# A new hand-written issue order for all engines of a cross-attention kernel

## The chip, the cores and the metric

The kernel runs on one core of a Trainium2 chip. The metric is the device time of one execution in microseconds (us), from start to end of the program. An execution is also profiled, and the profile gives the span from its first to its last instruction.

## What is computed

The reference, cut to what matters (B = 32 batches, 512 query rows and 512 context rows of 512 features, 16 heads of 32, all float32):

```python
qn  = layer_norm(x, q_norm_g, q_norm_b)
kvn = layer_norm(ctx_1024, kv_norm_g, kv_norm_b)
Q = (qn @ Wq).reshape(B, 512, 16, 32).transpose(0, 2, 1, 3)
K = (kvn @ Wk).reshape(B, 512, 16, 32).transpose(0, 2, 1, 3)
V = (kvn @ Wv).reshape(B, 512, 16, 32).transpose(0, 2, 1, 3)
attn = softmax(einsum('bhqd,bhkd->bhqk', Q, K) / sqrt(32))
ctx = einsum('bhqk,bhkd->bhqd', attn, V).transpose(0, 2, 1, 3).reshape(B, 512, 512)
out = x + gelu(ctx @ Wo + bo, approximate=False)
```

## The kernel before, in words

The program is one software pipeline, unrolled over the batches -1 to 32. A batch has four steps, one for each group of four heads (a "unit"). Each engine walks its own list of short names, `ORDER[engine][step]`, and waits on semaphores where a name needs another engine's result. So the lists alone set which work stands ahead of which on an engine. `known(b)` and `valid(b)` drop names that have no batch to work on. In batch -1, the head, only loads, normalisation, weight preparation and the first products exist; `PLAN_OF_HEAD` sorts its steps 2 and 3 a little differently.

The names on TensorE (PE):

- `q`, `k`, `v`, `o`: one sixth of a projection of 512 columns, two matmuls each (12 for a projection, because each float32 operand is split in a high and a low part of type fp32r, L868). In step s, `q` and `k` belong to the unit two steps ahead.
- `s`: one score block of the next unit, which is only reduced to its row maximum (L896, evicted by VectorE, L718, also named `s`). `st`: one transposed score block of the current unit (L888, evicted by ScalarE with the exponential, L575, also named `st`). Sixteen of each in a step, all in one rotation of four PSUM banks (`score`): a score matmul waits until the score block four places before it has been evicted.
- `m`: transposes the maxima when VectorE has reduced all 16 blocks (`md`, L777). It starts a short chain: ScalarE `mh` (L625), VectorE `ml` (L783), ScalarE `mx` four times (L629), and then the next step's first `st` may run.
- `pv`: 16 column-tiled matmuls, probabilities times V (L916), two in a step. `z`: 8 matmuls for the softmax sums (L859), which wait for six additions on GpSimd (`add`, L487).
- `x`: four transposes of a normalised tile (L956), eight in step 1. `x` on ScalarE and VectorE are the copies out of PSUM (L600, L694).

The projections, `x`, `m` and `z` share three PSUM banks (`gen`), taken in rotation in the order in which they are listed; the next user of a bank waits for the last one's eviction.

The other names: `ln`, `la`, `lv` (VectorE, L737 to L749) and `ln` (GpSimd, L503, L506) are the layer norm's statistics, and `norm` (ScalarE, L596) applies them. `q` and `k` on ScalarE (L606, L620) and VectorE (L696) evict the two parts of a projection, which SyncE then spreads by DMA into `q_stack` and `k_stack` (`rq`, `rk`). `rz` copies zero rows into `q_stack`. `ob` (VectorE, L759) adds the output bias, `gelu` (ScalarE, L592) follows, `res_add` (GpSimd) adds the residual, `store` and `res` are its transfers. `zt`, `zr`, `zb`, `cn` normalise the context, `split` cuts it in its two parts. `stack_used` tells that all `st` of a step are done, so that a stack's slot may be written again.

Of the kernel before, what the change touches and what calls it, by code (L numbers as in the profile page):

```python
# [19 lines left out]
NU = HEADS // HU  # L20
# [40 lines left out]
    ),  # L61
    "act": (
# [4 lines left out]
    ),  # L67
    "dve": (
        "s ln s*2 ln s la ln q ln s la s la zt zr lv s zb lv*2 cn la s*9 md ml ln k ob",
        "ln la lv la ln q lv zt zr zb ln la x s lv s cn lv s*2 k x s x la s lv x*2 s*4 x s*2 x ob s*2 x s*2 "  # L70
        "md ob ml",
        "s*5 ob s*2 zt s zr zb s cn s*4 k s*3 md q ml",
        "k zt zr zb cn s*2 q s*14 md ml",
    ),
    "pool": (
        "ln*3 split add*6 ln*3 res_add",
        "ln add ln add*3 res_add add res_add add split",
        "add*6 split res_add",
        "split add*6",
    ),  # L80
    "sp": (
        "load*6 rz rq load*2 rk store res",
        "rz rq rk",
        "store res rz rk rq store first_res",
        "rk store rq rz first_res",
# [94 lines left out]
def build(nc, x, ctx_in, q_g, q_b, kv_g, kv_b, wq, wk, wv, wo, bo, out):  # L180
    B = x.shape[0]
    zero_rows = nc.dram_tensor("zero_rows", (SHIFTS, HU * D), F32).ap()
    with ExitStack() as es:
# [21 lines left out]
        res = sb("res", [P, 2, D])  # L205
# [27 lines left out]
        ctx_ps = ps("ctx")  # L233
# [60 lines left out]
        def known(b):  # L294
            return isinstance(b, int)
# [5 lines left out]
        def valid(b):  # L301
            return not known(b) or 0 <= b < B
# [81 lines left out]
        def _(sp):  # L384
# [23 lines left out]
            def batch(b):  # L408
                PLAN = plan_of(b)
                for s in range(NU):  # L410
# [4 lines left out]
                    for kind, n, part in PLAN["sp"][s]:  # L415
                        if kind == "load" and valid(b + 1):
                            load_tile(b + 1, n)
                        if kind == "rz" and valid(b2):
# [5 lines left out]
                        if kind in ("rq", "rk") and valid(b2) and not (kind == "rq" and known(b) and (b, s) == (-1, 2)):  # L424
                            which = kind[1]
                            wait(sp, free[which], NU * b2 + u2 + 1)
                            wait(sp, stack_used, NU * b2 + u2 + 1)
# [577 lines left out]
```

## Time and profile before

| | us |
|---|---|
| median of 3 runs | 3231.49 |
| lowest, highest | 3231.26, 3232.49 |
| the profiled execution's own time | 3231.49 |
| its span, first to last instruction | 3229.7 |
| mean granted TensorE clock | 0.997 of full speed |

The profiled execution is the median itself, and 1.8 us of it lie outside the span. In the profile a group of instructions is named by its line and by what it writes and reads. "Idle before" is the time for which the engine stood still just ahead of an instruction, and the arrow names what ended it.

### The profile page before, as it was taken

How to read it: one execution, taken by the hardware profiler on the slowest of the kernel's cores; microseconds unless marked ns; L12 is line 12 of the kernel's file. 1: busy time of each engine (PE TensorE's matmuls, PEld its weight loads, DVE VectorE, ACT ScalarE, POOL GpSimd, SP SyncE). 2: the span in 40 equal slices, each digit the busy share in tenths (PEclk: the TensorE clock that was granted, in tenths of full speed). 3: DMA queues.
4: the chain of work that ended last, by engine and by line, in shares of the span. 5: the costliest groups of instructions: out<-in, count | busy, mean ns of one | idle time of the engine just before them, and what ended most of it. 6: DMA issues, size and time to landing. Idle time of an engine off the chain costs nothing.

```text
span 3229.7 us, 50112 instructions
## 1 busy us (share of the span) xinstructions
PE 3196.3 (99%) x16611; PEld 2148.0 (67%) x16611; DVE 2274.2 (70%) x4769; ACT 2306.6 (71%) x3985; POOL 2318.6 (72%) x1544
## 2 busy tenths in 40 slices
PE   8999999999999999999999999999999999999998
PEld 5566666666666666666666666666666666666664
DVE  6677677677677776776776777766767767777664
ACT  4677767777767777677777677776777776777765
POOL 2677677777777777777777777777777777777775
PEclk9999999999999999999999999999999999999999
DMA  4445445345444354453454444544534544544442
GB/s 147 101 104 129 115 119 133 95 115 137 115 115 120 104 130 115 120 133 95 115 136 116 115 119 105 130 115 121 131 95 115 138 115 114 121 105 128 115 102 79
DMA packets 193010, 376.85 MB, mean 117 GB/s; under 512 B 22625, under 2 KB 22641, under 8 KB 188658
## 3 DMA queue, kind: packets, MB, share of 16 engines
q1 hardware_dynamic: 192288, 372.86, 45.2%
q8 instruction: 134, 2.20, 0.3%
q14 instruction: 122, 1.00, 0.1%
q10 hardware_dynamic: 466, 0.80, 0.1%
HBM read 138.42 MB, written 33.82 MB: 53 GB/s over the span
## 4 chain that ended last, share of the span: by engine, by line
PE 98%; DVE 1%; ACT 1%; issue 0%; DMA 0%; ACTq 0%; POOL 0%
PE gen L868 43%; PE score L896 15%; PE score L888 15%; PE ctx L916 15%; PE gen L859 4%; PE gen L956 3%; PE gen L978 1%; DVE maxes L718 1%; PE score L800 0%; ACT probs L575 0%; PE gen L849 0%; ACT q_stack L629 0%; PE score L849 0%; ACT tok L596 0%; PE score L827 0%
## 5 line engine op out<-in xcount | busy, mean ns | idle before, releaser
L487 POOL TENSOR_TENSOR probs<-probs 128x1024 f32<-128x1024 f32 x762 | 1806.5, 2405 | 430.1 <-PE ctx L916 426.2
L718 DVE TENSOR_REDUCE maxes<-score 128x1 f32<-128x512 f32 x2048 | 1304.0, 681 | 267.8 <-PE score L896 256.7
L575 ACT ACTIVATE probs<-score 128x512 f32<-128x512 f32 x2048 | 1083.5, 606 | 229.7 <-PE score L888 219.9
L896 PE MATMUL score<-k_stack,q_stack 128*128 128x512 f32 x2048 | 728.7, 404 | 0.8 <-DVE maxes L718 0.2
L888 PE MATMUL score<-q_stack,k_stack 128*128 128x512 f32 x2048 | 713.9, 401 | 6.4 <-ACT q_stack L629 5.1
L896 PEld LDWEIGHTS score<-k_stack,q_stack 128*128 128x128 f32 x2048 | 380.0, 188 | 216.2 <-issue 81.1
L888 PEld LDWEIGHTS score<-q_stack,k_stack 128*128 128x128 f32 x2048 | 377.8, 188 | 185.6 <-ACT probs L575 42.4
L916 PE MATMUL ctx<-probs,v_sb 128*32 128x512 f32 x4096 | 492.4, 598 | 0.6 <-ACT probs L575 0.5
L868 PE MATMUL gen<-cT,w_k 128*128 128x512 f32 x1536 | 451.9, 399 | 0.1
L868 PE MATMUL gen<-xT,w_q 128*128 128x512 f32 x1536 | 444.0, 395 | 0.0
L868 PE MATMUL gen<-w_v,cT 128*128 128x512 f32 x1536 | 443.8, 390 | 0.0
L868 PE MATMUL gen<-w_o,ctx_hl 128*128 128x512 f32 x1488 | 401.5, 394 | 0.0
L503 POOL TENSOR_TENSOR rstd<-var_eps,minus_half 128x1 f32<-128x1 f32 x256 | 142.1, 555 | 322.5 <-DVE neg_mean L749 322.5
L696 DVE SCALAR_TENSOR_TENSOR k_nat<-gen,bias_k,k_nat 128x512 fp32r<-128x512 f32 x128 | 95.8, 749 | 357.9 <-ACT k_nat L620 357.9
L629 ACT ACTIVATE q_stack<-max_hl,chunk_mask 32x512 fp32r<-32x512 f32 x512 | 326.3, 706 | 29.7 <-DVE max_hl L783 28.2
L868 PEld LDWEIGHTS gen<-cT,w_k 128*128 128x128 f32 x1536 | 283.4, 191 | 80.1 <-DVE q_nat L696 27.0
L868 PEld LDWEIGHTS gen<-w_v,cT 128*128 128x128 f32 x1536 | 288.8, 188 | 62.6 <-issue 0.8
L868 PEld LDWEIGHTS gen<-xT,w_q 128*128 128x128 f32 x1536 | 288.7, 190 | 59.0
L868 PEld LDWEIGHTS gen<-w_o,ctx_hl 128*128 128x128 f32 x1488 | 274.9, 188 | 56.7
L916 PEld LDWEIGHTS ctx<-probs,v_sb 128*32 128x32 f32 x4096 | 109.3, 109 | 230.6 <-issue 206.8
L514 POOL TENSOR_TENSOR ctx_hl<-ctx_n,ctx_hl 128x512 fp32r<-128x512 f32 x128 | 164.9, 1288 | 99.8 <-ACT ctx_hl L581 99.7
L586 ACT ACTIVATE v_sb<-gen 128x512 f32<-128x512 f32 x128 | 76.1, 594 | 220.7 <-PE gen L868 220.7
(89 smaller groups left out, 2720.9 us busy)
## 6 DMA issues: line engine op xcount, KB each, us to landing
k_stack<-k_nat SPq DMA_DIRECT2D x384, 256.0 KB, 4.2
q_stack<-q_nat SPq DMA_DIRECT2D x381, 256.0 KB, 5.1
tok<-in_x SPq DMA_DIRECT2D x132, 256.0 KB, 6.0
tok<-in_ctx SPq DMA_DIRECT2D x128, 256.0 KB, 6.3
q_stack<-zero_rows SPq DMA_DIRECT2D x128, 256.0 KB, 3.3
res<-in_x SPq DMA_DIRECT2D x124, 256.0 KB, 2.6
out<-res SPq DMA_DIRECT2D x124, 256.0 KB, 2.5
probs<-in_L_xattn_Wq SPq DMA_DIRECT2D x1, 1024.0 KB, 8.5
```

The source lines that it names most:

```text
L487: pool.tensor_tensor(probs[:, c + 1, heads], probs[:, c + 1, heads], probs[:, c, heads], ALU.add).then_inc(pool_added, 1)
L503: pool.tensor_tensor(rstd[:, n:n + 1], var_eps[:, n:n + 1], minus_half[:], ALU.pow).then_inc(ln_rstd, 1)
L514: pool.tensor_tensor(ctx_hl[:, 1, up], ctx_n[:], raw(ctx_hl[:, 0, up]), ALU.subtract).then_inc(ctx_split, 1)
L575: act.activation(probs[:, n, part, :], score_at(s, "st", i)[:], ACT.Exp, scale=SCALE).then_inc(exp_done, 1)
L629: act.activation(q_stack[SROW:P, u1 % 2, :, P * n:P * (n + 1)], raw(max_hl[SROW:P, :]).unsqueeze(1).to_broadcast([SHIFTS, HU, P]), ACT.Ide ...
L718: dve.tensor_reduce(maxes[:, u1 % 2, SROW + i:SROW + i + 1], score_at(s, "s", i)[:], AX_X, ALU.max, negate=True).then_inc(max_done, 1)
L859: mm = pe.matmul(bank[DH * j:DH * (j + 1), :], ones[:, 0:DH], probs[:, c, j, :], start=(i == 0), stop=(i == len(chunks) - 1))
L868: mm = pe.matmul(bank[:, :], stationary(hs, c), moving(hm, c), start=(i == 0), stop=(i == len(TERMS) * NC - 1))
L888: pe.matmul(score_bank(pe, b, s, "st", i)[:, :], k_stack[:, s % 2, part, P * n:P * (n + 1)], q_stack[:, s % 2, part, :], start=True, stop= ...
L896: pe.matmul(score_bank(pe, b, s, "s", i)[:, :], q_stack[:, u1 % 2, n, P * part:P * (part + 1)], k_stack[:, u1 % 2, n, :], start=True, stop ...
L916: mm = pe.matmul(ctx_ps[DH * j:DH * (j + 1), :], v_sb[:, c, lo:lo + DH], probs[:, c, j, :], start=(c == 0), stop=(c == NC - 1))
L956: mm = pe.matmul(bank[:, P * c:P * (c + 1)], tok[:, n, P * c:P * (c + 1)], ident[:], start=True, stop=True, is_transpose=True)
```

## The change

All engines' lists are written anew. Per step nearly the same names stand in them; their sequence differs. One `o` goes from step 1 to step 2 on TensorE, one `ln` and one `lv` from step 1 to step 0 on VectorE, one `res_add` from step 2 to step 1 on GpSimd; on SyncE stores and residual loads change steps. The name `rz` is gone: the transfer of zero rows is issued where `rq` stands, ahead of the q restack, with one wait on `stack_used` for both. The copy of the output bias on VectorE, once in the program, moves from the start of step 0 of batch 0 into `prepare`, which is called ahead of the first `q` or `k` of a step.

```diff
     "pe": (
-        "q*3 v*2 s q s q s v st*2 v st q st s st v st*2 v s v*2 st s st z s st*2 v st v*2 s*2 v st s pv st s "
-        "st s k st s*2 o s*2 pv m k*5 o*3",
-        "o st*4 o st q*4 st q*2 st*2 x z k st k st k st k st s k s x k st s*2 st x pv st s st s x*2 pv s*3 x "
-        "s x s o s o*3 x o*2 s*2 o*4 s*2 o*4 m",
-        "o s o s*4 o s k o s k*2 st*2 k st z s q st*2 q st*2 k s st k st*2 s st q s pv s st*3 q st s q s st q "
-        "s*2 pv m",
-        "k*3 q k q k v st*2 k st*2 q st*2 v st q st q*2 st*4 z st*3 s v*2 st s*2 pv s*3 v s v s v*2 s*3 v s "
-        "v*2 s*2 v s*2 pv m",
+        "q*3 v q*2 v q v st*2 v*2 s st v st s st v*2 st s st s z v st*3 s v*2 st*2 s st k v s*4 pv st s st*2 o s "
+        "st s k s*2 pv m k o*2 k o k*2",
+        "o st*2 o st*3 q st q*4 st q st*3 z x k*3 x st*2 x st k*2 s k st s st*2 pv s x s x s x s pv s x s*2 o*3 "
+        "s*2 x o s o*2 s o s o*2 s o s o*3 m",
+        "o*4 s o s k s k s st k s st z st s st s st q st q st s s st*2 k st*3 k s st k st*4 pv s*2 q s q s*2 q s*2 q "
+        "pv m",
+        "k q k v q v k*2 st*3 k st*2 q st*2 k q st q st q st*2 z st*4 v st v s*3 pv s*2 v s*2 v s*2 v s v s*2 v*2 "
+        "s*2 v s*2 v pv m",
     ),
     "act": (
-        "st*5 q st*4 v st*3 split st v st*3 norm*2 mh norm mx*4 k",
-        "st*5 gelu q st*4 x st*3 x st norm st k x norm st*2 x*2 norm*3 x*3 gelu mh gelu mx*4 split",
-        "gelu st*11 k st*5 q split mh mx*4",
-        "st*7 k st*8 q split st v*2 mh mx*4",
+        "q st*4 v st*8 norm v split norm*2 st*4 mh mx*4 k",
+        "st*6 gelu q st x st*2 norm st*4 x k st*2 norm x norm st x*2 norm x norm x*2 gelu mh gelu mx*4 split",
+        "gelu st*12 k split st*4 q mh mx*4",
+        "st*6 k st*5 q st*4 split st v*2 mh mx*4",
     ),
     "dve": (
-        "s ln s*2 ln s la ln q ln s la s la zt zr lv s zb lv*2 cn la s*9 md ml ln k ob",
-        "ln la lv la ln q lv zt zr zb ln la x s lv s cn lv s*2 k x s x la s lv x*2 s*4 x s*2 x ob s*2 x s*2 "
-        "md ob ml",
-        "s*5 ob s*2 zt s zr zb s cn s*4 k s*3 md q ml",
-        "k zt zr zb cn s*2 q s*14 md ml",
+        "q s ln s*2 la ln lv s ln s la*2 zt s zr lv zb s cn ln lv s la s*3 lv s*5 md ml ln*2 k ob",
+        "ln la*2 q zt lv*2 x la zr ln zb cn lv s la x k lv s x s*2 x*2 s*2 x s*3 x s*2 x s ob s*4 md ob ml",
+        "s ob s*6 zt s zr zb s cn s k s*7 md q ml",
+        "k zt zr zb cn q s*16 md ml",
     ),
     "pool": (
-        "ln*3 split add*6 ln*3 res_add",
-        "ln add ln add*3 res_add add res_add add split",
-        "add*6 split res_add",
+        "ln*3 split add*6 res_add ln*3",
+        "ln*2 add*5 res_add add res_add split res_add",
         "split add*6",
+        "add split add*5",
     ),
     "sp": (
-        "load*6 rz rq load*2 rk store res",
-        "rz rq rk",
-        "store res rz rk rq store first_res",
-        "rk store rq rz first_res",
+        "load*8 rq rk store res",
+        "rq rk store res store",
+        "store first_res rk rq first_res",
+        "rq rk",
     ),
...
-                        if kind == "rz" and valid(b2):
+                        if kind == "rq" and valid(b2):
...
                             wait(sp, free[which], NU * b2 + u2 + 1)
-                            wait(sp, stack_used, NU * b2 + u2 + 1)
                             if which == "q":
                                 restack(sp, u2, q_nat, q_stack, ((0, 0), (1, 0), (2, 1)), q_stacked)
                             else:
+                                wait(sp, stack_used, NU * b2 + u2 + 1)
                                 restack(sp, u2, k_nat, k_stack, ((0, 0), (1, 1), (2, 0)), k_stacked)
```

## Rows read from the trace of the kernel before

**Rows 1.** Busy time in one batch: PE, PEld, DVE, ACT, POOL; then clock, DMA share, GB/s.

```profile
1006.58:1105.40 98.82, 98.81 (x517) 66.57 (x516) 70.52 (x149) 71.71 (x124) 72.70 (x49) 1.00 0.46 118
```

**Rows 2.** TensorE's timeline in one batch of the steady stretch: start, length, what.

```profile
1006.58 0.27 PE L978 MATMUL gen<-ident,maxes 128*128 128x128 f32 x1
...
1011.50 0.61 PE L888 MATMUL score<-q_stack,k_stack 128*128 128x512 f32 x2
...
1012.73 1.06 PE L859 MATMUL gen<-probs,ones 128*32 128x512 f32 x8
1013.72 0.50 PE L896 MATMUL score<-k_stack,q_stack 128*128 128x512 f32 x1
...
1030.39 0.66 PE L888 MATMUL score<-q_stack,k_stack 128*128 128x512 f32 x2
...
1039.32 0.61 PE L896 MATMUL score<-k_stack,q_stack 128*128 128x512 f32 x2
...
1072.50 0.33 PE L978 MATMUL gen<-ident,maxes 128*128 128x128 f32 x1
...
1074.97 1.98 PE L868 MATMUL gen<-w_o,ctx_hl 128*128 128x512 f32 x8
1076.79 1.11 PE L888 MATMUL score<-q_stack,k_stack 128*128 128x512 f32 x4
...
1082.40 1.06 PE L859 MATMUL gen<-probs,ones 128*32 128x512 f32 x8
...
1105.40 0.27 PE L978 MATMUL gen<-ident,maxes 128*128 128x128 f32 x1
```

**Rows 3.** ScalarE's timeline, step 3 of that batch.

```profile
1030.92 3.54 ACT L575 ACTIVATE probs<-score 128x512 f32<-128x512 f32 x7 [0.65 <-PE score L888]
1034.48 0.69 ACT L620 ACTIVATE k_nat<-gen,bias_k 128x512 fp32r<-128x512 f32 x1
1035.07 4.25 ACT L575 ACTIVATE probs<-score 128x512 f32<-128x512 f32 x8
```

**Rows 4.** ScalarE's timeline at the start of step 2.

```profile
1010.63 0.63 ACT L581 ACTIVATE ctx_hl<-ctx_n 128x512 fp32r<-128x512 f32 x1 [0.18 <-PE gen L868]
1011.53 0.60 ACT L592 ACTIVATE act_out<-gen 128x512 f32<-128x512 f32 x1 [0.27 <-DVE gen L759]
1013.44 4.92 ACT L575 ACTIVATE probs<-score 128x512 f32<-128x512 f32 x9
```

**Rows 5.** VectorE's timeline, the last part of step 1.

```profile
1092.84 0.68 DVE L694 TENSOR_TENSOR xT<-gen,xT 128x512 fp32r<-128x512 f32 x1
...
1095.78 2.49 DVE L718 TENSOR_REDUCE maxes<-score 128x1 f32<-128x512 f32 x4 [0.27 <-PE score L896]
...
1101.04 0.70 DVE L759 TENSOR_TENSOR gen<-gen,bias_all 128x512 f32<-128x512 f32 x1 [0.38 <-PE gen L868]
...
1104.88 0.17 DVE L777 TENSOR_REDUCE maxes<-maxes 128x16 f32<-128x16 f32 x1
```

**Rows 6.** GpSimd's timeline: the six additions of step 0.

```profile
1067.67 14.19 POOL L487 TENSOR_TENSOR probs<-probs 128x1024 f32<-128x1024 f32 x6 [0.53 <-PE ctx L916]
```

**Rows 7.** VectorE's timeline in the head: first statistics, first variance.

```profile
5.56 1.28 DVE L737 BATCH_NORM_STATS2 stats<-tok 128x6 f32<-128x512 f32 x2
...
8.23 0.12 DVE L748 TENSOR_SCALAR var_eps<-moments 128x1 f32<-128x1 f32 x1
```

**Rows 8.** TensorE's timeline: head and batch 0.

```profile
12.96 1.97 PE L956 MATMUL gen<-ident,tok 128*128 128x128 f32 x8 [1.63 <-DVE xT L694]
...
17.75 1.86 PE L800 MATMUL score<-probs,norm_cols 128*1 128x512 f32 x2
...
89.66 1.75 PE L888 MATMUL score<-q_stack,k_stack 128*128 128x512 f32 x5 [1.55 <-ACT q_stack L629]
...
118.42 0.30 PE L978 MATMUL gen<-ident,maxes 128*128 128x128 f32 x1 [3.38 <-DVE maxes L777]
```

**Rows 9.** The page's DMA issues: size of one, and us to landing.

```profile
k_stack<-k_nat SPq DMA_DIRECT2D x384, 256.0 KB, 4.2
```

More of the change, by code:

```diff
@@ L689, in prepare @@
                     low_weights(3, "o", None)
+                if (b, s) == (0, 0):
+                    dve.wait_ge(bo_mm, 1)
+                    dve.tensor_copy(bias_all[:], ctx_ps[:]).then_inc(bo_ready, 1)
+                    dve.wait_ge(bo_ready, 1)
             def low_part(dst, psum, hi, done, bias=None):
@@ L705, in batch @@
                     t1, t2, tp = NU * b1 + u1, NU * b2 + u2, NU * bp + up
-                    if known(b) and (b, s) == (0, 0):
-                        dve.wait_ge(bo_mm, 1)
-                        dve.tensor_copy(bias_all[:], ctx_ps[:]).then_inc(bo_ready, 1)
-                        dve.wait_ge(bo_ready, 1)
                     for kind, n, part in PLAN["dve"][s]:
```

3 rows, old and new, of the table ORDER are left out of this document.

## The prediction, made before the changed kernel was built or run

> **What bounds the kernel now.** I read the windows first. In one batch of the steady stretch, 98.82 us long, TensorE is busy for 98.81; VectorE, ScalarE and GpSimd are busy for 70 to 73 us [rows 1]. The clock is at 1.00. So TensorE sets the time, and what it does in a batch does not depend on the sequence of its names: 192 projection matmuls, 128 scores, 8 `pv`, 4 `z`, 8 `x`, 4 `m` before and after. The counts per step differ by one `o` alone. With no wait to remove inside, a new order can hardly gain there; what it can do is make a wait. "72% busy" does not say how near that is. So I next put the timelines of the engines beside each other and looked for margins: how long before TensorE reaches a name is the result that it needs ready. They are small everywhere, some tenths of a us, and each number below is such a margin, recomputed for the new lists. Last I read the head and batch 0, where TensorE does stand still.
>
> Prices on TensorE, from rows: eight matmuls of 512 columns take 1076.79 - 1074.97 = 1.82 us, so 0.228 each: a score costs 0.23, a token of `q`, `k`, `v` or `o` (two matmuls) 0.455 [rows 2]. A `z` takes 1013.72 - 1012.73 = 0.99, and I add 0.2 for the slower start of it and of what follows (the row behind it is 0.50 long and not 0.39 as others): 1.2 [rows 2].
>
> **Terms, step by step.** All are for one steady batch; about 30 batches are full.
>
> (a) Start of a step. Behind `m` the next step's first `st` waits for ScalarE's four `mx`. Before, step 0 to 1 has 8 tokens and a `norm` between `mh` and `mx`; now 7 tokens and the `o` of step 1, so 8 again, and no `norm`. Nothing lost: 0.
>
> (b) End of step 1. The last `m` waits for 16 reductions. Before, from VectorE's third `x` at 1092.84 there stand 6 `x`, 11 `s`, one `ob` and small ones, and VectorE still idles 0.27 and 0.38 us, and `md` ends at 1104.88 + 0.17 = 1105.05, 0.35 ahead of `m` at 1105.40 [rows 5, 2]. So some 1.0 us are spare. Now 14 `s` stand behind the third `x`, at 0.60 each (four of them take 2.49 us with an end of 0.68, [rows 5]): 3 x 0.60 = 1.8 more, 0.2 less for one `la` and `lv`. TensorE needs two tokens less between the two `m`: 1105.40 - 1072.50 = 32.90 becomes 31.99. The third `x` copy comes earlier, because ScalarE's list has one `norm` less before it and no `norm` before `mx`: I add up the new ScalarE list (an exponential (3.54 - 0.6) / 6 = 0.49 [rows 3]; `x` at 0.5 and `norm` at 0.7, estimates on both sides of `k`'s 0.59) and get 18.9 us behind the first `m` where it was 1092.84 - 1072.50 = 20.3. VectorE's rest is then 14 x 0.60 + 6 x 0.60 + 0.6 + 0.2 = 12.8, ready at 31.8 for 31.99. The margin is 0.2 at best, and no idle time is left in VectorE's row of work to absorb a late copy. I take a loss of 0.1; bounds 0 and 0.5.
>
> (c) Step 3, a score bank. The third `s` ahead of the first `pv` takes the bank of the 15th `st`. Before: the first `st` starts at 1030.39, ScalarE works from 1030.92 on, seven exponentials, `k` (0.59 until the next starts), eight exponentials, and the 15th ends at 1035.07 + 4.25 = 1039.32 [rows 3]. That `s` is the second matmul of the row at 1039.32, so at 1039.55: margin 0.23 [rows 2]. The `q` eviction stood behind all of them. Now it stands ahead of the last five: 0.59 more, at `k`'s price. TensorE's path between the same two is the same set, 16 `st`, 2 `s`, 8 tokens, one `z`, again 9.16 us. ScalarE had idled in the row of eight (7 x 0.49 + 0.6 = 4.0 of its 4.25), so 0.25 is absorbed. Loss: 0.59 - 0.25 - 0.23 = 0.1, and up to 0.3 if the idle time isn't all usable. I take 0.2; bounds 0 and 0.36. The Trainium skill, "TensorE: Matmul & The Clock Gate", section "Architectural detail", says that ScalarE's and VectorE's queues are strictly first in, first out, and this rule speaks against the change: an eviction that nobody needs soon holds up those behind it. If the engine could pass `q` by, the term would be nothing; the trace shows no instruction passing another on ScalarE, and the sum goes by the rows.
>
> (d) Step 2, score banks. TensorE reaches the first `st` 1011.50 - 1006.58 = 4.92 us behind `m` [rows 2], and ScalarE's first exponential starts at 6.86, because `split`, `gelu` and a table load come first [rows 4]. Now three `s` and one `k` less and one `o` more stand ahead of the first `st`: 4.92 - 0.69 + 0.0 = 4.23. ScalarE gets earlier too: `split` waited 0.18 for the last `o`, which is now the fifth token and not behind seven `s`, and `gelu` waited 0.27; with both gone and the 0.1 to 0.2 between them the first exponential starts at 6.2 to 6.4 and ends 0.6 later, at 6.8 to 7.0. The score four places on comes at 4.23 + 3 x 0.23 + 0.455 + 1.2 + 0.23 = 6.8. Loss 0 to 0.2; I take 0.1.
>
> (e) `z` of step 1 waits for six additions: they end at 1067.67 + 14.19 = 1081.86, 0.54 ahead of `z` at 1082.40 [rows 6, 2]. Between the first `pv`, which releases them, and `z` one token less stands now: 0.54 - 0.455 = 0.09. No loss, but no room. The three other `z` lose 0.45 to 0.9 of their margins in the same way. Together with the `gelu` that moved behind a sixth exponential: 0.05, bounds 0 and 0.3.
>
> (f) SyncE. Zero rows now leave just ahead of the q restack, and the k restack has no transfer but these ahead of it in steps 1 and 3. A restack of k lands 4.2 us after its issue [rows 9], and the first `s` that reads it stands over 7 us of TensorE's work behind in every step. Hidden: 0. If that cover went it would cost the landing time less what is left of the cover, some us in a batch; nothing points there. The bias copy is at the same place in effect, since the first name in VectorE's step 0 is now `q`: 0.
>
> (g) The head. VectorE's first `lv` starts at 8.23, behind four statistics and three `la`; now behind two statistics and one `la`: two statistics at 0.6 each (two take 1.28) and small ones earlier, 1.3 us [rows 7]. All that follows it on GpSimd and ScalarE up to the first transpose moves with it. Further, the second `x` stood three places behind the first in the rotation of three banks (`x z k .. x`) and so waited 1.63 us for its copy [rows 8]; now `z x k x x` gives it another bank. I take 1.2 of that. From 17.75 on [rows 8] no gap stands in TensorE's timeline for 40 us, so what it starts earlier there counts in full: -2.5; bounds 0 (the weights come too late) and -3.5.
>
> (h) Batch 0 and the end. With no `o` to do, TensorE waits for `mx` before the first `st` of step 1 for 1.55 us and for the maxima at its end for 3.38 us [rows 8]. The first had 5 tokens of `k` as cover and now has 4, less 0.45 for the `norm`: 0.0 to +0.45. The second is VectorE's and grows as in (b), by up to 1 us. In step 3 of the head four `v` stand ahead of the first `s` and not two: 0.4 to 0.9 later. Together +1.0. In batch 31 step 2 has no `k` and `q` between its scores, and all seven last `s` come behind the first `pv`: +0.7. Sum +1.7, bounds 0 and 3.
>
> **Sum.** Steady: 0.1 + 0.2 + 0.1 + 0.05 = 0.45 us a batch, times 30 = 13.5; head -2.5; ends +1.7; in all +12.7. The profiled execution took 3231.49, which is the median of the runs itself, so 3244.
>
> **Rivals.** *The margins hold* (chance 0.27): every term (b) to (e) is nothing, because each is a difference of some tenths between long sums. What speaks for it: each has a lower bound at or near 0. Then 3231.5 - 2.5 + 1.7 = 3231, within 0.2%. *The other side, a faster steady stretch* (0.12): between the first `st` of step 3 and the `s` of (c) TensorE took 9.16 us where its prices make 18 x 0.228 + 8 x 0.455 + 1.2 = 8.94; there and elsewhere some 0.2 us a batch are waits too short to show as idle. If the new lists remove them and add none, 30 x 0.2 = 6 and the head's 2.5 are gained, less 1.7: 3225, or 3222 with the head's full bound; it decides if (b) and (c) both keep a margin. *One long wait in every batch* (0.20): VectorE's unbroken run in (b) starts late, since the third `x` copy stands behind two exponentials and a `norm` on ScalarE, and all its 22 instructions push `m`, while `m`'s chain pushes the next step; with 0.5 there, 0.36, 0.2 and 0.3 in the others 1.0 to 1.4 a batch is lost: 3261 to 3273. *The restack is late* (0.03): 1 us or more a batch, over 3262.
>
> **How the numbers follow.** My forecast has 0.38. Two times in ten lie outside 3227 to 3263: most of the long-wait case's upper half, the late restack, and the better half of the faster one. The forecast's own range is 3236 to 3254. A difference of 0.2%, 6.5 us, is about what a measurement of this kernel can tell from no change. Slower by more: nearly all of 0.38, 0.20 and 0.03, together 0.58. Within: the 0.27 and some of the faster case, 0.31. Faster: 0.11.
>
> **What would show it.** In the profile after: batches 0.3 to 0.6 us longer than the 98.8 of before [rows 1]; VectorE without idle gaps in the last 13 us of step 1, and `m` right behind `md`; in step 3 `s` behind the 15th exponential; the first variance at about 7 us and the stretch at 17.75 beginning near 15. Batches of the old length would refute (b) to (e), a head of the old length (g). I am wrong above all if the copies and evictions whose place I counted start earlier than I count.

## The result, and the profile after

| us | before | after |
|---|---|---|
| median of 4 runs | 3231.99 | 3255.86 |
| lowest, highest | 3231.26, 3232.49 | 3254.92, 3257.0 |
| span of the profiled execution | 3229.7 | 3252.7 |

The kernel is slower: the ratio is 1.0075, with a 95% interval of 1.0056 to 1.0092. That is 23.9 us more where I had forecast 12.5 more (3244 for 3231.5). The sign holds and the size is nearly twice my sum. The time lies inside 3227 to 3263, outside of which I had put two chances in ten, but above the forecast's own 3236 to 3254: it falls between that range and the 3261 to 3273 of the long wait. The profiled execution of the changed kernel took 3254.48 us and is not one of the four in the table.

One correction to the text ahead of the prediction. Three added lines of its diff were copied wrongly. The first line of TensorE's step 0, the first line of its step 2 (here with the second behind it), and VectorE's step 2 read in the changed kernel:

```
"q*3 v q*2 v q v st*2 v*2 s st v s st s v*2 st s st s z v st*3 s v*2 st*2 s st k v s*4 pv st s st*2 o s "
"o*4 s o s k s k s st k s st z st s st s q st q st s st*2 k st*3 k s st k st*4 pv s*2 q s q s*2 q s*2 q "
"pv m",
"s ob s*6 zt s zr zb cn s k s*7 md q ml",
```

No working of the prediction rests on a name in which the wrong and the right lines differ. In the changed kernel these lines have a number lower by one: L895 is `s`, L887 `st`, L867 the products, L717 the reductions. The `x` copies on VectorE are L697.

The same windows view as [rows 1], one batch of the kernel after, from the `m` of step 1 to the next one:

```profile
1008.74:1108.24 99.50, 99.46 (x516) 65.91 (x517) 69.82 (x149) 70.93 (x124) 72.56 (x49) 1.00 0.45 117
```

The batch is 99.50 us long where it was 98.82, at the same clock, and TensorE still shows as busy for all but 0.04 of it. The batch holds the same matmuls. So the lost time doesn't appear as idle time of the matmuls, and the view of waits agrees. For the kernel after, between 170 and 3100 us, it lists not one wait of a TensorE matmul. Its first lines for the whole program (us in total, times, longest) are all in the head and the ends:

```profile
PE score L887 <- ACT q_stack L628: 6.9, 3, 3.4
...
PE gen L977 <- DVE maxes L776: 4.2, 3, 2.2
```

The same view of the engine's weight loads (PEld), which run beside the matmuls, does show where to look. Between 170 and 3100 us, loads of `s` and `st` wait for an exponential on ScalarE 60 times in the kernel before and 298 times in the kernel after. Before, and then after:

```profile
PEld score L888 <- ACT probs L575: 33.8, 59, 0.8
...
PEld score L896 <- ACT probs L575: 0.3, 1, 0.3
```

```profile
PEld score L895 <- ACT probs L574: 76.9, 173, 0.8
...
PEld score L887 <- ACT probs L574: 41.6, 125, 0.8
```

The us of these lines are not the loss, because a load that waited can still be in time for its matmul.

I therefore cut each batch at its four `m` and took the distances between their starts in TensorE's timeline, as means over 25 batches of the steady stretch. A step's distance changes also because work changed sides of an `m`: by matmul counts, step 0 has 2 product matmuls more (0.455 us), step 1 has 4 less (0.91) and step 2 has 2 more. The last column takes that out.

| step | before | after | lost |
|---|---|---|---|
| 0 | 21.82 | 22.35 | 0.08 |
| 1 | 32.89 | 32.17 | 0.19 |
| 2 | 20.00 | 20.79 | 0.34 |
| 3 | 23.94 | 24.23 | 0.29 |
| batch | 98.65 | 99.55 | 0.90 |

The budget of the span: 30 batches lose 27; the first `m` comes at 59.13 us and not at 62.61, which gives 3.5 back; batch 0 is 98.29 long and not 99.86, 1.6 less; the last batch loses 1.2. In all +23.1, and the spans differ by 23.0.

TensorE's timeline after, for the same places as [rows 2] (the `m` of steps 1, 0 and 1, and what stands ahead of some names):

```profile
1008.74 0.30 PE L977 MATMUL gen<-ident,maxes 128*128 128x128 f32 x1
...
1013.88 0.49 PE L887 MATMUL score<-q_stack,k_stack 128*128 128x512 f32 x1
1014.29 1.07 PE L858 MATMUL gen<-probs,ones 128*32 128x512 f32 x8
1015.29 0.50 PE L887 MATMUL score<-q_stack,k_stack 128*128 128x512 f32 x1
1015.74 0.51 PE L895 MATMUL score<-k_stack,q_stack 128*128 128x512 f32 x1
1016.08 0.40 PE L887 MATMUL score<-q_stack,k_stack 128*128 128x512 f32 x1
...
1041.98 1.17 PE L895 MATMUL score<-k_stack,q_stack 128*128 128x512 f32 x3
1043.08 1.92 PE L915 MATMUL ctx<-probs,v_sb 128*32 128x512 f32 x16
...
1076.09 0.33 PE L977 MATMUL gen<-ident,maxes 128*128 128x128 f32 x1
...
1084.76 0.84 PE L887 MATMUL score<-q_stack,k_stack 128*128 128x512 f32 x3
1085.64 1.07 PE L858 MATMUL gen<-probs,ones 128*32 128x512 f32 x8
...
1108.24 0.30 PE L977 MATMUL gen<-ident,maxes 128*128 128x128 f32 x1
```

Read the distances between starts, not the lengths. Three `s` at 1041.98 should hand over to `pv` after 3 x 0.23 and some 0.09 for the change of tile, 0.78; they take 1.10, so 0.32 is lost there. From the `s` at 1015.74 to the `st` at 1016.08 it is 0.34 for a matmul that otherwise takes 0.23. Matmuls whose weights were not loaded ahead are 0.49 to 0.51 long (that behind a `z` too, in both kernels), others 0.39.

What holds them is seen on the engine's second row, the weight loads (start, length, idle time of the loads before it, and what ended it), in step 2 and step 3:

```profile
1013.86 0.19 PEld L887 LDWEIGHTS score<-q_stack,k_stack 128*128 128x128 f32 x1 [0.25 <-DVE maxes L717]
...
1015.74 0.19 PEld L895 LDWEIGHTS score<-k_stack,q_stack 128*128 128x128 f32 x1 [0.26 <-ACT probs L574]
...
1041.76 0.19 PEld L895 LDWEIGHTS score<-k_stack,q_stack 128*128 128x128 f32 x1
1042.16 0.19 PEld L895 LDWEIGHTS score<-k_stack,q_stack 128*128 128x128 f32 x1 [0.21 <-ACT probs L574]
1042.65 0.19 PEld L895 LDWEIGHTS score<-k_stack,q_stack 128*128 128x128 f32 x1 [0.30 <-ACT probs L574]
```

The weights of the first `s`, at 1041.76, are loaded 0.22 us ahead of its matmul. Those of the third, at 1042.65, wait for an exponential, and the matmul then starts together with them: 1041.98 + 1.17 = 1043.15 is its end, 0.50 behind 1042.65. So a semaphore that a matmul waits for holds its weight load too. Here is the same place in ScalarE's timeline, which answers to [rows 3], ahead of it the start of step 2, which answers to [rows 4]:

```profile
1015.09 2.07 ACT L574 ACTIVATE probs<-score 128x512 f32<-128x512 f32 x4
...
1037.53 2.54 ACT L574 ACTIVATE probs<-score 128x512 f32<-128x512 f32 x5
1039.91 0.73 ACT L605 ACTIVATE q_nat<-gen,bias_q 128x512 fp32r<-128x512 f32 x1
1040.48 2.12 ACT L574 ACTIVATE probs<-score 128x512 f32<-128x512 f32 x4
```

The `q` eviction takes 0.57 until the next starts, and the last exponential ends at 1040.48 + 2.12 = 1042.60, and the load starts 0.05 behind it. At the start of step 2 the first exponential starts 15.09 - 8.74 = 6.35 behind `m`, inside the 6.2 to 6.4 that I worked out in (d).

The end of step 1 on VectorE (answers to [rows 5]), then the six additions on GpSimd (answers to [rows 6]):

```profile
1095.24 0.69 DVE L697 TENSOR_TENSOR xT<-gen,xT 128x512 fp32r<-128x512 f32 x1 [0.67 <-ACT xT L599]
...
1105.41 2.47 DVE L717 TENSOR_REDUCE maxes<-score 128x1 f32<-128x512 f32 x4
1107.92 0.17 DVE L776 TENSOR_REDUCE maxes<-maxes 128x16 f32<-128x16 f32 x1
```

```profile
1071.32 14.17 POOL L486 TENSOR_TENSOR probs<-probs 128x1024 f32<-128x1024 f32 x6
```

From the third `x` copy at 1095.24 on VectorE's timeline shows no idle gap until `md` ends at 1108.09, and `m` follows 0.15 behind it. The additions end at 1085.49, and `z` starts 0.15 behind them. Both are as (b) and (e) said.

### The profile page after: what moved, and what is told of

It reads as the page before. It is cut to its first block, busy times and chain, and to the rows that moved or that the text cites. A ratio compares the mean times of both kernels' runs of the same rounds, so it can differ in the third digit from the quotient of the medians.

```text
span 3252.7 us, 49985 instructions
## 1 busy us (share of the span) xinstructions
PE 3221.7 (99%) x16611; PEld 2124.3 (65%) x16611; DVE 2255.8 (69%) x4769; ACT 2281.0 (70%) x3985; POOL 2315.2 (71%) x1544
## 4 chain that ended last, share of the span: by engine, by line
PE 97%; DVE 1%; ACT 1%; issue 1%; POOL 0%; DMA 0%; ACTq 0%; POOLq 0%; DVEq 0%
PE gen L867 42%; PE score L895 15%; PE score L887 15%; PE ctx L915 14%; PE gen L858 4%; PE gen L955 4%; PE gen L977 1%; DVE maxes L717 1%; ACT probs L574 0%; ACT q_stack L628 0%; PE score L799 0%; DVE stats L736 0%; PE gen L848 0%; POOL probs L486 0%; PE score L848 0%
## 5 line engine op out<-in xcount | busy, mean ns | idle before, releaser
L717 DVE TENSOR_REDUCE maxes<-score 128x1 f32<-128x512 f32 x2048 | 1295.6, 682 | 217.2 <-PE score L895 215.1
L895 PE MATMUL score<-k_stack,q_stack 128*128 128x512 f32 x2048 | 757.9, 411 | 2.8 <-DVE maxes L717 1.9
L887 PE MATMUL score<-q_stack,k_stack 128*128 128x512 f32 x2048 | 695.5, 406 | 7.1 <-ACT q_stack L628 6.9
L895 PEld LDWEIGHTS score<-k_stack,q_stack 128*128 128x128 f32 x2048 | 377.3, 188 | 226.6 <-ACT probs L574 83.4
L887 PEld LDWEIGHTS score<-q_stack,k_stack 128*128 128x128 f32 x2048 | 373.6, 188 | 203.2 <-DVE maxes L717 68.2
L867 PE MATMUL gen<-cT,w_k 128*128 128x512 f32 x1536 | 459.7, 398 | 0.2 <-DVE q_nat L699 0.2
L867 PE MATMUL gen<-w_v,cT 128*128 128x512 f32 x1536 | 458.1, 393 | 0.0
L867 PE MATMUL gen<-xT,w_q 128*128 128x512 f32 x1536 | 446.9, 393 | 0.0
L867 PE MATMUL gen<-w_o,ctx_hl 128*128 128x512 f32 x1488 | 416.0, 395 | 0.0
L867 PEld LDWEIGHTS gen<-w_v,cT 128*128 128x128 f32 x1536 | 286.0, 188 | 81.0 <-issue 26.8
L867 PEld LDWEIGHTS gen<-xT,w_q 128*128 128x128 f32 x1536 | 288.0, 189 | 60.1
L867 PEld LDWEIGHTS gen<-cT,w_k 128*128 128x128 f32 x1536 | 286.7, 192 | 53.5 <-DVE q_nat L699 1.1
L867 PEld LDWEIGHTS gen<-w_o,ctx_hl 128*128 128x128 f32 x1488 | 275.7, 189 | 55.3
```

The lines of the kernel that those rows point to most:

```text
L717: dve.tensor_reduce(maxes[:, u1 % 2, SROW + i:SROW + i + 1], score_at(s, "s", i)[:], AX_X, ALU.max, negate=True).then_inc(max_done, 1)
L867: mm = pe.matmul(bank[:, :], stationary(hs, c), moving(hm, c), start=(i == 0), stop=(i == len(TERMS) * NC - 1))
L887: pe.matmul(score_bank(pe, b, s, "st", i)[:, :], k_stack[:, s % 2, part, P * n:P * (n + 1)], q_stack[:, s % 2, part, :], start=True, stop= ...
L895: pe.matmul(score_bank(pe, b, s, "s", i)[:, :], q_stack[:, u1 % 2, n, P * part:P * (part + 1)], k_stack[:, u1 % 2, n, :], start=True, stop ...
```

## The experiments

Step lengths are means as in the table above, and "batch" is their sum. Ratios are to runs of the kernel before that were taken beside each experiment; their medians were 3231.45, 3230.15 and 3232.52 us, so the ratios compare better than the times.

### One place of ScalarE's `q` eviction, taken back

Edit on the changed kernel, ScalarE's step 3:

```diff
-        "st*6 k st*5 q st*4 split st v*2 mh mx*4",
+        "st*6 k st*9 q split st v*2 mh mx*4",
```

> The changed kernel, with ScalarE's q eviction in step 3 put back behind the last exponential but one place as in the kernel before (st*6 k st*9 q). Local theory: each late result costs TensorE what the trace shows at its place, and in step 3 the third s ahead of pv starts 0.205 us late, the pv behind it 0.11 and an st before them 0.04. So a batch gets 0.3 us shorter, 99.55 to about 99.25, and the whole about 9 to 10 us faster than the changed kernel (3246). Rival, the long wait: the time is set by one run of work on VectorE and the chain behind m, so that the next wait takes over; then the batch stays above 99.45 and the whole above 3252.

Measured: 3253.86 us, ratio to before 1.0067 (1.0052 to 1.0082); step 3 24.16 and not 24.23, batch 99.49. The third `s` ahead of `pv` stands now 0.25 behind the second and not 0.43, so that wait is gone. But two later `s` of the step come 0.06 and 0.11 later. VectorE's own `q` stands ahead of its 16 reductions in the changed list (`q s*16`), and it needs ScalarE's `q` first. One wait was removed and the one behind it took most of the time.

### Both lists of step 3 put back

Edit on the changed kernel, ScalarE and VectorE, step 3:

```diff
-        "st*6 k st*5 q st*4 split st v*2 mh mx*4",
+        "st*6 k st*9 q split st v*2 mh mx*4",
...
-        "k zt zr zb cn q s*16 md ml",
+        "k zt zr zb cn s*2 q s*14 md ml",
```

> The changed kernel with q late on ScalarE in step 3 as before, and in addition two of VectorE's reductions put ahead of its own q (s*2 q s*14, as in the kernel before). With q late on ScalarE alone, step 3 came back by 0.1 us only; two s late in it, 0.06 and 0.11, are new, since VectorE's q, which waits for ScalarE's, stands ahead of all 16 reductions. Theory: that was the second wait, and step 3 goes from 24.24 to 24.0 us; the batch to 99.3. Rival: with the z, the pv and the last s of step 3 still late, less than 0.12 comes back.

Measured: 3247.12 us, ratio 1.0054 (1.0037 to 1.0071); step 3 24.00, batch 99.32. Step 3 is back to 0.06 of what it was before (23.94), with TensorE's and GpSimd's new lists in place. So the loss of step 3 is the place of the `q` eviction on the two engines, and not TensorE's own sequence.

### The early `q` eviction alone, in the kernel before

```diff
-        "st*7 k st*8 q split st v*2 mh mx*4",
+        "st*7 k st*3 q st*5 split st v*2 mh mx*4",
```

Here `q` stands ahead of six of the 16 exponentials, in the changed kernel ahead of five; the 12th to the 15th are behind it in both.

> The kernel before with that one edit made alone: in step 3 ScalarE evicts q ahead of the last five exponentials (st*3 q st*5), 0.59 us of work more ahead of them. By the prediction's sum (margin 0.23 and idle time 0.25 before it counts) the batch gets 0.1 us longer, 98.66 to 98.76, the whole +3. Theory of the hidden margin: a wait that ends last still shows 0.12 to 0.15 us between release and start, so the real margin was 0.1 and the batch gets 0.25 to 0.35 longer, 98.9 to 99.0, the whole +8 to +11. Rival, that the other lists must change too for it to count: no change.

Measured: 3247.72 us, ratio 1.0046 (1.003 to 1.0063); step 3 24.44 (+0.50), batch 99.20. The cost is five times my sum, and well over what a hidden margin of 0.1 makes of it. The timelines show why: it isn't the `s` of (c) that is late most, but one that needs the 12th exponential, three before. ScalarE's timeline, then TensorE's:

```profile
1042.79 0.71 ACT L606 ACTIVATE q_nat<-gen,bias_q 128x512 fp32r<-128x512 f32 x1
1043.36 2.58 ACT L575 ACTIVATE probs<-score 128x512 f32<-128x512 f32 x5
```

```profile
1043.42 1.11 PE L888 MATMUL score<-q_stack,k_stack 128*128 128x512 f32 x3
1044.62 0.47 PE L896 MATMUL score<-k_stack,q_stack 128*128 128x512 f32 x1
```

The `s` at 1044.62 needs the bank of the second exponential behind `q`, the last of the three `st` ahead of it that of the first. The `s` comes 0.35 late, that `st` 0.09, and what follows 0.08.

### The same, with `q` moved ahead of the 15th exponential alone

```diff
-        "st*7 k st*8 q split st v*2 mh mx*4",
+        "st*7 k st*7 q st split st v*2 mh mx*4",
```

> The kernel before with q on ScalarE in step 3 moved ahead of one exponential only, the 15th, the one whose bank the prediction counted. Ahead of five it made step 3 0.50 us longer (24.44), not the 0.1 to 0.3 counted. If the loss came from the 15th exponential, it is 0.59 - 0.23 = 0.36 here, and step 3 24.3. If it came from the banks of the 11th and 12th, which stand ahead of ScalarE's idle 0.12 us and have less margin, those are free here and the 15th alone gives 0.36, so the same number, but the late instruction is the s of the 15th and none before it. If the margin hides a fixed time between release and start of 0.05 to 0.12, it is 0.41 to 0.48, step 3 24.35 to 24.4.

Measured (one execution): 3245.43 us; step 3 24.42 (+0.48), batch 99.14. The 16th exponential was behind `q` before as well, so ahead of `pv` only the `s` of (c) can be late. TensorE's matmuls and weight loads there, and ScalarE:

```profile
1042.63 0.39 PE L896 MATMUL score<-k_stack,q_stack 128*128 128x512 f32 x1
1043.24 0.50 PE L896 MATMUL score<-k_stack,q_stack 128*128 128x512 f32 x1 [0.23 <-ACT probs L575]
1043.67 0.64 PE L916 MATMUL ctx<-probs,v_sb 128*32 128x512 f32 x4
```

```profile
1042.40 0.19 PEld L896 LDWEIGHTS score<-k_stack,q_stack 128*128 128x128 f32 x1
1043.24 0.19 PEld L896 LDWEIGHTS score<-k_stack,q_stack 128*128 128x128 f32 x1 [0.65 <-ACT probs L575]
```

```profile
1042.01 0.69 ACT L606 ACTIVATE q_nat<-gen,bias_q 128x512 fp32r<-128x512 f32 x1
1042.58 0.61 ACT L575 ACTIVATE probs<-score 128x512 f32<-128x512 f32 x1
```

The exponential ends at 1043.19 and the load starts 0.05 later, at 1043.24. The matmul was due at 1042.63 + 0.23 = 1042.86, so it starts 0.38 late, and `pv` follows it after 0.43 and not 0.35, which is 0.08 more. Both parts count: 0.46. My margin arithmetic gives 0.57 - 0.23 = 0.34 for it.

The weight load of the same `s` in the kernel before shows the rest:

```profile
1039.36 0.19 PEld L896 LDWEIGHTS score<-k_stack,q_stack 128*128 128x128 f32 x1
```

Its matmul starts at 1039.55 [rows 2], and the 15th exponential ended at 1039.32 [rows 3]. So even there the load had started right behind that exponential, some 0.05 us, and it was only 0.19 ahead of the matmul. The `q` of 0.57 took these 0.19, and the load had to be 0.11 ahead: 0.57 - (0.19 - 0.11) = 0.49, and the step lost 0.48.

### Step 3 alone

All four engines' new lists of step 3, and nothing else, in the kernel before:

```diff
-        "k*3 q k q k v st*2 k ...
+        "k q k v q v k*2 st*3 k ...
...
-        "st*7 k st*8 q split st v*2 mh mx*4",
+        "st*6 k st*5 q st*4 split st v*2 mh mx*4",
...
-        "k zt zr zb cn s*2 q s*14 md ml",
+        "k zt zr zb cn q s*16 md ml",
...
-        "split add*6",
+        "add split add*5",
```

> The kernel before with the changed lists of step 3 on TensorE, ScalarE, VectorE and GpSimd, all else as before. Step 3 lasts 23.93 us from m to m before and 24.24 after. Local theory: 24.2 to 24.3 here too, the other three steps as before (21.8, 32.9, 20.0), batch 98.97, the whole about +9 us. Rival, long wait: step 3 depends on the steps ahead of it, and it stays below 24.1.

Measured: 3241.78 us, ratio 1.0031 (1.002 to 1.0042); step 3 24.25, the others 21.83, 32.90 and 20.03, batch 99.00. This step's loss is made inside it, and no other step pays or gains.

### Step 2 undone, and undone with GpSimd

On the changed kernel, the lists of before for step 2 on TensorE (with the `o` that had come from step 1), ScalarE and VectorE:

```diff
-        "gelu st*12 k split st*4 q mh mx*4",
+        "gelu st*11 k st*5 q split mh mx*4",
...
-        "s ob s*6 zt s zr zb cn s k s*7 md q ml",
+        "s*5 ob s*2 zt s zr zb s cn s*4 k s*3 md q ml",
```

> The changed kernel, with step 2 on TensorE, ScalarE and VectorE as in the kernel before (one o more, since the changed lists hold it there). In the trace of the changed kernel step 2 has z 0.10 late, three scores 0.09, 0.11 and 0.03 late. Local theory: step 2 goes from 20.79 to 20.45 (19.99 of before and the one o, 0.455), the batch from 99.55 to 99.2, the whole 10 us faster than the changed kernel. Rival: the late work moves into step 3 or to m, and less than 0.1 a batch comes back.

Measured: 3455.37 us, ratio 1.069 (1.0674 to 1.0706); step 2 20.48, but step 3 30.80. The forecast was 10 us below the changed kernel; I had overlooked the third engine. GpSimd's timeline, and then all waits of TensorE between 300 and 3100 us:

```profile
1085.98 1.28 POOL L513 TENSOR_TENSOR ctx_hl<-ctx_n,ctx_hl 128x512 fp32r<-128x512 f32 x1 [11.82 <-ACT ctx_hl L580]
1087.21 14.08 POOL L486 TENSOR_TENSOR probs<-probs 128x1024 f32<-128x1024 f32 x6
```

```profile
PE gen L858 <- POOL probs L486: 92.7, 26, 3.6
PE score L887 <- ACT probs L574: 29.7, 26, 1.2
```

GpSimd's changed list of step 2 has `split` ahead of its six additions, and ScalarE's `split`, which it waits for, stood now at the end of ScalarE's list. GpSimd stands idle for 11.8 us ahead of its own, and the additions start 20.8 us behind the `m` that opens step 2, where it is 15.6 in the changed kernel. `z` waits for them in every batch (26 times), 3.6 us, and an `st` ahead of it for an exponential, 1.1 us. That is 4.7 of the 6.6 us that step 3 grew by; TensorE's granted clock falls behind the wait of `z` as well, to 0.50 from 1101.44 to 1104.80, its level of 1.2 GHz. This run says nothing of step 2's own cost. It shows what a list on one engine may cost when its partner's list is another's: 7.2 us a batch over the kernel before, against the 0.9 of the whole change.

With GpSimd's list put back as well:

```diff
-        "split add*6",
+        "add*6 split",
```

> The run with step 2 undone once more, now with GpSimd's list of step 2 put back too (add*6 split for split add*6). In that run step 2 took 20.47 us as expected and step 3 30.8, because z waited for GpSimd: split stood ahead of the six additions there, and ScalarE's half of split at the end of its list. Local theory: step 2 20.47 again, step 3 back at 24.24, batch 99.25 against 99.55 of the changed kernel, the whole 9 us below it, near 3246. Rival, that undoing step 2 only moves the wait: step 3 at 24.4 or more.

Measured: 3243.04 us, ratio 1.004 (1.0025 to 1.0055); steps 22.35, 32.18, 20.48, 24.24, batch 99.24. Step 2 is at 20.00 + 0.455 + 0.02. Its whole loss is in the lists of step 2. No run takes its two waits, named under (d) below, apart.

### Steps 0 and 1 alone

The last kernel, with the step 3 of before on all four engines. What is left of the change are steps 0 and 1, the `o` that they gave to step 2, the head, and SyncE's lists:

```diff
-        "st*6 k st*5 q st*4 split st v*2 mh mx*4",
+        "st*7 k st*8 q split st v*2 mh mx*4",
```

> The changed kernel with steps 2 and 3 of the kernel before on TensorE, ScalarE, VectorE and GpSimd (one o more in step 2), so that only steps 0 and 1 and SyncE's list are changed. Local theory, steps are independent: 22.35, 32.15, 20.45 and 23.93 from m to m, batch 98.9 (0.25 over the kernel before), head and batch 0 as in the changed kernel; the whole 3231.5 + 30 x 0.25 - 3.5 - 1.5 = 3234. Rival: what was late in steps 2 and 3 came from steps 0 and 1, then batch 99.3 or more.

Measured: 3234.05 us, ratio 1.0012 (1.0002 to 1.0021); steps 22.31, 32.17, 20.46, 23.94, batch 98.88. By batches, the three parts add up: 98.88 - 98.65 = 0.23 for steps 0 and 1 and SyncE, 99.00 - 98.65 = 0.35 for step 3, 99.55 - 99.24 = 0.31 for step 2; together 0.89 for 0.90.

### The head alone

The kernel before, with the changed order of statistics and normalisation in batch -1 only:

```diff
+HEAD_LISTS = {
+    "act": ("norm*3", "x norm x norm x norm x*2 norm x norm x*2", ORDER["act"][2], ORDER["act"][3]),
+    "dve": ("ln la ln lv ln la*2 lv ln lv la lv ln*2", "ln la*2 lv*2 x la ln lv la x lv x*6", ORDER["dve"][2], ORDER["dve"][3]),
+}
```

> The kernel before, but in batch -1, the head, VectorE and ScalarE go by the changed lists' order of layer norm and x (first variance behind two statistics and not four); TensorE's order there and the rotation of the three banks are as before, and so is every other batch. By the prediction's term (g) the first m, at 62.61 us before and 59.13 in the changed kernel, comes 1.3 us earlier from this part, 61.3, and the banks are the other part; batches stay at 98.65; the whole 1.3 us faster, within noise of no change. Rival: the banks alone hold the head up, then the first m stays at 62.6.

Measured: 3228.06 us, ratio 0.9995 (0.9986 to 1.0005); first `m` at 60.35 where it was 62.61. Then the same with TensorE's step 1 changed to give the second `x` another bank:

```diff
-        "o st*4 o st q*4 st q*2 st*2 x z k st k ...
+        "o st*4 o st q*4 st q*2 st*2 z x k st k ...
```

> The kernel before with the changed head order on VectorE and ScalarE and, in step 1 of TensorE's list, z x k instead of x z k, so that the first two x no longer share a bank. Prediction's term (g): 1.2 us come from the banks; the first x copies then run on and the first m comes at 59.1 to 59.6, as in the changed kernel (59.13), where the order alone gave 60.35. Price in every batch: z stands one x (0.45 us) nearer to GpSimd's additions, 0.54 before and 0.09 after, and by the trace of the changed kernel, where 0.15 is left, such a z starts 0.09 late: batch 98.75, the whole 3226 + 3 - 1 = 3228. Rival: the bank costs nothing once the variances come early, first m at 60.3.

Measured: 3229.24 us, ratio 0.9991 (0.9982 to 1.0); first `m` at 59.24, batch 98.67, so the early `z` costs nothing in the steady stretch. TensorE's timeline in the head, of the first of these kernels, of the second, and of the changed kernel:

```profile
8.67 1.12 PE L960 MATMUL gen<-ident,tok 128*128 128x128 f32 x4 [3.52 <-ACT tok L600]
11.80 3.68 PE L960 MATMUL gen<-ident,tok 128*128 128x128 f32 x16 [2.02 <-DVE xT L698]
15.42 1.01 PE L804 MATMUL score<-probs,norm_cols 128*1 128x512 f32 x1
```

```profile
8.58 2.07 PE L960 MATMUL gen<-ident,tok 128*128 128x128 f32 x8 [3.52 <-ACT tok L600]
11.71 2.82 PE L960 MATMUL gen<-ident,tok 128*128 128x128 f32 x12 [1.06 <-DVE xT L698]
14.46 1.76 PE L804 MATMUL score<-probs,norm_cols 128*1 128x512 f32 x2
```

```profile
11.47 2.82 PE L955 MATMUL gen<-ident,tok 128*128 128x128 f32 x12 [1.06 <-DVE xT L697]
14.22 1.54 PE L799 MATMUL score<-probs,norm_cols 128*1 128x512 f32 x2
```

With the other bank, a second set of four transposes goes ahead of the wait, and the wait falls from 2.02 to 1.06. Everything behind stands 0.96 earlier (15.42 to 14.46), of which 0.10 is that VectorE's first statistics start at 5.18 and not at 5.28. So the head's gain has the two causes that (g) names.

### The bank of `z` in step 3

In the kernel before, the `st` ahead of `z` in step 3 is followed 0.11 late. To learn whether `z` waits there for the bank that `k`'s eviction frees, that eviction was put one exponential earlier (beside the head's edit):

```diff
-        "st*7 k st*8 q split st v*2 mh mx*4",
+        "st*6 k st*9 q split st v*2 mh mx*4",
```

> The kernel before with the changed head order on VectorE and ScalarE (first m 60.4 instead of 62.6 us, measured alone) and, in step 3, ScalarE's k eviction ahead of one exponential (st*6 k st*9 q). In the kernel before z of step 3 starts 0.11 us late and the st ahead of it 0.05, each batch, and the bank of z is the one that k leaves last. Local theory: step 3 goes from 23.93 to 23.8, the batch from 98.65 to 98.5, and the whole to 3226 or below, 0.15% under the kernel before. Rival: z waits for GpSimd's additions and not for the bank, or the exponential pushed behind k makes another score late; then step 3 stays at 23.9 or grows.

Measured: 3233.69 us, ratio 1.0 (0.9991 to 1.0009); step 3 23.94, as before, batch 98.74. The forecast of 23.8 is refuted: it is not `k`'s bank. What stays is a score bank of the `st` itself. In the kernel before, at 1134.53, the weight load of that `st` has waited 0.31 for an exponential, and the edit left as much work ahead of that one; no run isolated the place.

## Why the prediction had half of the loss

**The bound** was right. TensorE is the one engine that sets a batch, and its matmuls show neither an idle time that could have been removed nor one that was made. Where the loss sits shows in the waits of its weight loads. In the kernel before they showed already which margins were short, and I did not use them. The rivals of a faster steady stretch and of margins that hold are refuted: a batch is 0.90 longer.

**(a), start of a step: forecast 0, measured 0.08 in step 0.** No distance in that step grew by over 0.05 us; this remainder stays open. The count behind (a) was off: at the change from step 0 to step 1 nine tokens stood ahead of the first `st` before (eight behind `m` and the `o` of step 1) and eight now, so that it starts 3.82 behind `m` and not 4.28, and the distances show no loss from it.

**(b) and (e), step 1: forecast 0.15, measured 0.19.** The working held to 0.3 us: the third copy starts 1095.24 - 1076.09 = 19.15 behind `m` (forecast 18.9), VectorE's run without a gap takes 12.85 (12.8), and `md` ends at 32.00 (31.8). The sixth addition ends 0.15 ahead of `z` (0.09). The distance from the last `o` to `m` is 0.60, 0.14 more than a free one, and that from `st` to `z` 0.09 more. The rival of one long wait is refuted at this place. Its mechanism exists (VectorE's unbroken run), its price is 0.14 and not 0.5. No run changed either place alone, so these two parts are read from the trace and not from an experiment.

**(c), step 3: forecast 0.2, measured 0.29.** The mechanism was right, and putting `q` back on both engines (24.00) shows it. The failed step is the sentence "at 1039.55: margin 0.23". I measured from the end of the exponential to the start of the matmul. But the release takes 0.05 to arrive, and the weight load, which waits for it as well, has to start 0.11 ahead of the matmul, so only some 0.07 was spare. The other two terms were right: the 15th exponential ends 13.09 behind the step's first `m` where it was 12.75 (means over the same 25 batches), 0.34 later for a `q` of 0.57, so 0.23 of idle time was absorbed (I had 0.25). And 0.34 - 0.07 = 0.27 is the loss to 0.02. The one-place run shows it in full: 0.38 and another 0.08, where the old arithmetic has 0.34. The early `q` in the kernel before (+0.50) shows a second mistake that only luck kept small here. I followed the bank of the 15th exponential alone. The eviction delays all those behind it, and what counts is the tightest bank among them.

**(d), step 2: forecast 0.1 with 0.2 as its bound, measured 0.34.** This is the largest miss. The path that I worked out was right: first exponential at 6.35 for 6.2 to 6.4, the score four places on due at 6.8. The failed step is the same as in (c): I set the end of the exponential (6.95) against the start of the matmul, with nothing for the way to the weight load and for its lead. The score got its load at 1015.74 - 1008.74 = 7.00. Behind that stand 0.09 for the late start and 0.11 for the load that was not ahead (to the `st` at 1016.08 it is 0.34 and not 0.23). And there is a second wait that I had not looked for. The `st` ahead of `z` waits for VectorE, which now does `ob` after one reduction and not after five; load at 1013.86, matmul at 1013.88, `z` 0.10 late. The three parts make 0.30 of the 0.34.

**(f), SyncE: forecast 0.** No restack shows in any wait of TensorE in the steady stretch: that rival is refuted.

**(g), head: forecast -2.5, measured -3.5, its bound.** The first variance starts at 6.34 us and not at 8.23 [rows 7] (forecast about 7), and the stretch of [rows 8] that began at 17.75 begins at 14.22 (forecast near 15). But VectorE's first statistics start at 4.94 and not at 5.56 [rows 7], and that start differs from one profiled execution to the next (4.86 to 5.93 over all runs). Counted from there, the stretch begins at 9.28 for 12.19, so the order gains 2.9: 2.05 by the statistics' order alone (10.14 in the first kernel with the new head; I had 1.3) and 0.86 by the bank (I had 1.2). The first `m` spreads more, with the clock: with the old head it stands at 61.23 and 61.43 in two kernels whose mean granted clock from 20 us to that `m` is 1.00, at 62.61 for 0.96 and at 64.89 for 0.92.

**(h), ends: forecast +1.7, measured -1.6 for batch 0 and +1.2 for the last.** The last batch's sum held to 0.5 (forecast 0.7). Batch 0's was compared over different clocks. The windows view of batch 0, for before, after, the head alone, and the head with `z` first:

```profile
62.61:162.47 99.86, 93.31 (x461) 60.53 (x461) 66.41 (x141) 63.89 (x115) 57.35 (x40) 0.95 0.36 83
```

```profile
59.13:157.42 98.29, 92.27 (x460) 58.48 (x460) 66.50 (x141) 63.35 (x115) 57.32 (x40) 0.97 0.36 83
```

```profile
60.35:158.69 98.34, 91.46 (x461) 59.25 (x462) 66.36 (x141) 63.88 (x115) 57.37 (x40) 0.97 0.37 85
```

```profile
59.24:158.88 99.64, 93.18 (x461) 60.40 (x462) 66.48 (x141) 63.87 (x115) 57.39 (x40) 0.95 0.36 84
```

At a mean granted clock of 0.97 batch 0 takes 98.34 in the old order and 98.29, 97.85 and 97.58 in the new one (the last two with step 2 undone and with the two lists of step 3 put back). At 0.95 it takes 99.64 and 99.86 in the old order (at 0.93, in the kernel of the last experiment, 101.81), and 98.90 and 99.12 in the new one (the first experiment, and steps 0 and 1 alone). In batch 0 the clock still falls from 2.4 to 1.2 GHz at times (before, its granted share is 0.50 from 64.0 to 67.4 us), and such stretches move its length by over 1 us. At the same clock the new order costs nothing there and is rather shorter; my +1.0 for it is refuted.

**The sum.** Steady 0.45 x 30 = 13.5 became 0.90 x 30 = 27; head and ends -0.8 became -3.9. That the total missed by no more than 11 us is in part luck: head and batch 0 gave back 3.6 us more than I had, and of that 0.6 is the earlier start of the first statistics and about 1 the clock in batch 0. The rule of the Trainium skill on ScalarE's queue ("TensorE: Matmul & The Clock Gate", section "Architectural detail"), cited at (c), agrees with the runs: with `q` ahead of a single exponential, that exponential started only 0.57 behind `q`'s start, and nothing passed.

## What to carry to other kernels

Where the bounding engine shows as fully busy, look at the waits of its weight loads, and compare the starts of the same instructions, step by step. A hold of a tenth of a us does not show as idle time and is multiplied by the batches. Measure a matmul's margin from the arrival of the release to where its weight load must start, and for each moved eviction check every bank that is freed behind it, not just one. And change partners together: an eviction's place on one engine is also a place on the engine that waits for it.

## What the runs showed of the hardware

I had not expected that a late release costs more than its lateness. For the 512-column fp32r matmuls of this kernel, the weight load starts 0.22 us ahead of its matmul when nothing holds it. Over all `s` and `st` behind a matmul of that shape in the steady stretch, before and after, a load 0.12 us or more ahead cost nothing. One only 0.08 ahead made the matmul 0.42 long and the next start come 0.26 behind it; one 0.04 ahead, 0.45 and 0.29; one that started together with its matmul (also behind `z` and `pv`), 0.50 and 0.335, where the undisturbed figures are 0.39 and 0.227. The end of the matmul stands 0.50 behind the start of its load in all of these. A load that waited started some 0.05 us behind the end of the eviction that released it (1042.60 and 1042.65, 1043.19 and 1043.24). So the spare time is some 0.16 us less than it looks between an eviction's end and a matmul's start, and each late release takes up to 0.11 on top of the matmul's late start.
